# Gate/up bias laid into PSUM by ScalarE, and expert outputs scattered to one DRAM row per (token, choice)

## The chip, the core and the metric

One core of one Trainium2 chip runs the whole program. TensorE (PE), VectorE (DVE), ScalarE (ACT), GpSimd (POOL) and SyncE (SP) each work off an instruction list of their own and wait for each other by semaphores; 16 DMA engines move data between DRAM and SBUF. The metric is the device time of one execution in microseconds (us), smaller is better.

## The reference

Four sequences of 256 tokens, 256 wide. First a causal 16-head attention of the normalised tokens over a context that is keys and values at once, added to `x`. Then a mixture of 16 experts on the normalised result, four experts a token:

```
x = x + attention(layernorm(x), ctx, ctx)
t = layernorm(x)                                   # 1024 tokens
top_val, top_idx = top_k(t @ router_weight.T + router_bias, 4)
score = softmax(top_val)
gate_up = t @ gate_up_proj[e] + gate_up_proj_bias[e]      # 256 -> 512, gate and up interleaved
gate = min(gate, 7); up = clip(up, -7, 7)
out_e = ((up + 1) * gate * sigmoid(1.702 * gate)) @ down_proj[e] + down_proj_bias[e]
x = x + sum over the token's four experts of score_e * out_e
```

## The kernel before

The program has four stages.

**Attention** (to about 108 us). `steps` is one list of units that all engines walk through: `T` transposes, `X` raw scores for the row maxima, `M` the maxima, `S` scores and exponentials, `V` weighing of values, `O` output, `Y` transposes of normalised tokens, `L` router logits, `R` ranks of tokens in their experts. `slot(b)` writes their order for each sequence `b`; the one for the last sequence is changed.

**Routing** (to about 136 us). The 4096 (token, choice) pairs are sorted into at most NB = 47 blocks of 128 slots, each block of one expert. Tables of zeros and single values (`vblk_hot`, `low_hot`) are multiplied on TensorE, and the product gives for every slot the token in it (`slot_tok`); a slot without a token gets a padding row. `down_rows(b)` multiplies scores by the down biases; ACT copies the result into `x_tok`. Normalised tokens with their scores go to `y_rows` in DRAM, and two DRAM tensors, `acc_rows0` and `acc_rows1`, are filled with `x1` (the tokens after attention) and with the bias rows.

**Blocks** (to about 302 us). For each block i POOL gathers 128 rows of `y_rows` by an indirect DMA (ring of 6, `xg`, a part of `ctx_tok`), PE transposes them (`x_turn`), multiplies by the gate/up weights (`gate_up`), DVE and ACT make the activation, PE transposes it (`h_turn`) and multiplies by the down weights (`down`), ACT scales by the score (`weighted`, into `o_sb`, a ring of 3 in `x_tok`), and POOL adds the 128 rows into `acc_rows` of the block's parity by an indirect DMA that adds; it first waits until the add two blocks earlier has landed. On PE the order of iteration i is `gate_up(i)`, `down(i-2)`, `h_turn(i-1)`, `x_turn(i+2)`; on ACT `sigmoid(i)`, `weighted(i-2)`, `h_turned(i-1)`, `x_turned(i+2)`; on POOL add(i), then gather(i+6). The gate/up bias comes from a matmul of its own ahead of the four weight matmuls of a block: a one-hot column picks the expert's row out of `bias_w`, the bias split into three bf16 parts.

**End.** The last LAST = 3 blocks are not scattered: `last_sum` adds them in PSUM by 24 matmuls with one-hot matrices. SP loads both accumulators (8 DMAs of 256 KB), DVE adds them, adds the PSUM sums, and SP writes `out`.

SP issues nearly all plain DMAs in one order. Lines that matter: L1525 bias matmul, L1529 gate/up, L1548 down, L1538 and L1507 transposes, L653 gather, L660 scatter, L1562 `last_sum`, L1482 bias rows, L498 loads of the accumulators, L1235 and L1240 final adds. The lines on which the order rests:

```
for i in range(NB):                       # POOL
    if i < NS: add_rows(i)
    if i + XG < NB: gather(i + XG)
```

## Time and profile before

| | us |
|---|---|
| median of 3 runs | 312.16 |
| lowest, highest | 309.71, 314.52 |
| the profiled execution | 314.45 |
| its span, first to last instruction | 312.70 |

| engine | busy us | share of the span |
|---|---|---|
| PE matmul | 274.2 | 88% |
| POOL | 185.8 | 59% |
| DVE | 179.8 | 57% |
| ACT | 134.4 | 43% |

A busy share is an average over stages; the block stage takes half the span and is the one to read row by row. The profile also has the clock that TensorE was granted (1.0 is 2.4 GHz, 0.5 is 1.2 GHz): it is 1.0 in the block stage and 0.5 over most of 93 to 140 us. Of the chain of work that ended last 61% is PE, 16% DVE, 5% DMA.

### The profile page before, as it was taken

To read this page: it belongs to the slowest core of one execution; us is meant where nothing else is said; L and a number is where in the kernel's file an instruction comes from. 1 tells how busy PE (TensorE), PEld (TensorE's weight loads), DVE (VectorE), ACT (ScalarE), POOL (GpSimd) and SP (SyncE) were. 2 spreads that over 40 slices of the span, in tenths; PEclk is the share of its full clock that TensorE was granted. 3 is DMA by queue.
4 is the path that set the end of the run, shared out by engine and by line. 5 is a ranking of instruction groups with operands and counts; after the bars stand their busy time and mean duration, and the time that the engine had idled before them with its cause. 6 is when DMAs were issued, how large, how long until landed. Compare 5 with 4: busy or idle time off the path is not lost.

```text
span 312.7 us, 5706 instructions
## 1 busy us (share of the span) xinstructions
PE 274.2 (88%) x1548; PEld 184.8 (59%) x1566; DVE 179.8 (57%) x476; ACT 134.4 (43%) x319; POOL 185.8 (59%) x228
## 2 busy tenths in 40 slices
PE   7696897698989868679998998999999999989895
PEld 6665475375576647335565664665666656556584
DVE  3897757966968477305453453544545556656533
ACT  3244564363464368323353443443444434434410
POOL 5873825624436846240876787687787777767300
PEclk9799999999995575559999999999999999999999
DMA  7704230010269395263454445354555545544574
GB/s 238 237 2 129 92 102 2 2 55 0 66 198 332 106 332 190 86 205 123 70 85 90 70 72 89 63 93 75 80 91 72 91 82 75 93 77 70 98 223 134
DMA packets 26877, 34.33 MB, mean 110 GB/s; under 512 B 2800, under 2 KB 21200, under 8 KB 26848
## 3 DMA queue, kind: packets, MB, share of 16 engines
q0 software_dynamic: 8592, 12.32, 24.0%
q1 hardware_dynamic: 17984, 21.39, 20.8%
q8 instruction: 15, 0.25, 0.3%
q10 hardware_dynamic: 272, 0.26, 0.2%
q14 instruction: 14, 0.11, 0.1%
HBM read 23.46 MB, written 10.43 MB: 108 GB/s over the span
## 4 chain that ended last, share of the span: by engine, by line
PE 61%; DVE 16%; issue 8%; DMA 5%; ACT 3%; POOL 3%; SPq 1%; another core or an unknown queue 1%; ACTq 0%; DVEq 0%
PE ps L1529 22%; PE ps L1548 9%; DVE neg_max L909 6%; PE ps L1265 4%; PE ps L1341 4%; PE ps L1562 3%; DMA ctx_tok<-y_rows,slot_tok 3%; PE ps L1507 3%; PE ps L1538 2%; PE ps L1525 2%; PE ps L1284 2%; DMA br_sb<-n_L_ffn_router_bias_dram 2%; PE ps L1343 2%; PE ps L1317 2%; DVE x_tok L941 1%
## 5 line engine op out<-in xcount | busy, mean ns | idle before, releaser
L1529 PE MATMUL ps<-w_all,q_norm 128*128 x188 | 90.3, 603 | 2.9 <-ACT q_norm L823 1.4
L660 POOL DMA_INDIRECT acc_rows<-x_tok,slot_tok x44 | 70.0, 1590 | 34.1 <-ACT x_tok L845 31.6
L1189 DVE TENSOR_SCALAR v_aug<-ps 128x256 f32<-128x256 f32 x47 | 20.0, 425 | 75.7 <-PE ps L1529 48.1
L653 POOL DMA_INDIRECT ctx_tok<-y_rows,slot_tok x47 | 46.6, 992 | 21.8 <-issue 13.7
L829 ACT ACTIVATE v_aug<-v_aug 128x256 f32<-128x256 f32 x47 | 19.6, 418 | 77.5 <-DVE v_aug L1189 77.5
L1548 PEld LDWEIGHTS ps<-w_all,o_t 128*128 128x128 f32 x188 | 35.6, 190 | 25.4 <-issue 22.9
L1529 PEld LDWEIGHTS ps<-w_all,q_norm 128*128 128x128 f32 x188 | 35.6, 194 | 25.0 <-issue 23.2
L1548 PE MATMUL ps<-w_all,o_t 128*128 x188 | 48.3, 380 | 1.1 <-ACT o_t L834 1.1
L564 POOL TENSOR_SCALAR_AFFINE_SELECT w_all<-w_all 128x256 f32<-128x256 f32 (+1 forms) x48 | 23.4, 505 | 37.1 <-ACT w_all L713 36.3
L713 ACT ACTIVATE w_all<-ps 128x512 f32<-128x512 f32 x48 | 25.5, 599 | 23.2 <-PE ps L1317 23.2
L909 DVE TENSOR_REDUCE neg_max<-ps 128x2 f32<-128x512 f32 (+1 forms) x48 | 30.5, 685 | 7.7 <-PE ps L1290 5.0
L845 ACT ACTIVATE x_tok<-ps,ctx_tok 128x256 f32<-128x256 f32 x47 | 22.3, 475 | 19.2 <-PE ps L1548 18.1
L1200 DVE TENSOR_TENSOR v_aug<-v_aug 128x256 f32<-128x256 f32 x47 | 20.0, 426 | 7.2 <-ACT v_aug L829 7.0
L1507 PE MATMUL ps<-ident,ctx_tok 128*128 128x128 f32 x94 | 19.0, 285 | 5.8 <-DMA ctx_tok<-y_rows,slot_tok 5.8
L1207 DVE SCALAR_TENSOR_TENSOR o_t<-v_aug 128x256 f32<-128x256 f32 x47 | 20.0, 426 | 4.3
L823 ACT ACTIVATE q_norm<-ps 128x256 f32<-128x256 f32 x47 | 18.1, 385 | 4.9 <-issue 4.0
L1284 PE MATMUL ps<-k_t,q_t 64*128 64x256 f32 (+1 forms) x128 | 13.4, 303 | 7.1 <-DVE neg_max L909 4.8
L1194 DVE TENSOR_SCALAR v_aug<-ps 128x256 f32<-128x256 f32 x47 | 19.5, 415 | 0.0
L1341 PE MATMUL ps<-w_all,v_aug 128*32 128x256 f32 x128 | 17.9, 450 | 1.5 <-ACT o_t L721 0.8
L1265 PE MATMUL ps<-ident,w_all 128*128 128x128 f32 x128 | 18.6, 295 | 0.0
L1538 PE MATMUL ps<-ident,o_t 128*128 128x128 f32 x94 | 17.9, 273 | 0.0
L834 ACT ACTIVATE o_t<-ps 128x256 f32<-128x256 f32 x47 | 17.7, 376 | 0.0
(160 smaller groups left out, 391.7 us busy)
## 6 DMA issues: line engine op xcount, KB each, us to landing
w_all<-_L_ffn_gate_up_proj_dram SPq DMA_DIRECT2D x16, 512.0 KB, 5.2
w_all<-in_L_ffn_down_proj_dram SPq DMA_DIRECT2D x16, 256.0 KB, 6.1
acc_rows<-x_tok SPq DMA_DIRECT2D x8, 256.0 KB, 8.2
x_tok<-in_x_dram SPq DMA_DIRECT2D x4, 256.0 KB, 4.8
y_ext<-acc_rows SPq DMA_DIRECT2D x4, 256.0 KB, 3.8
vblk_hot<-acc_rows SPq DMA_DIRECT2D x4, 256.0 KB, 3.7
out_dram<-y_ext SPq DMA_DIRECT2D x4, 256.0 KB, 2.2
ctx_tok<-in_ctx_dram SPq DMA_DIRECT2D x3, 256.0 KB, 5.6
```

The lines of the kernel that those rows point to most:

```text
L564: pool.affine_select(out=blk, in_=blk, compare_op=ALU.is_ge, fill=0.0, base=0, pattern=[[0, n], [1, P]], channel_multiplier=-1).then_inc(s ...
L653: pool.indirect_dma_start(out=xg[:, i % XG, :], out_offset=None, in_=y_dram[:, :], in_offset=bass.IndirectOffsetOnAxis(ap=slot_tok[:, i:i ...
L660: pool.indirect_dma_start(out=acc[i % 2][:, :], out_offset=bass.IndirectOffsetOnAxis(ap=slot_tok[:, i:i + 1], axis=0), in_=o_sb[:, i % 3, ...
L713: act.activation(prob[:, u % P_RING, :], ps[:, u % ST_RING, :], ACT.Exp, scale=SC).then_inc(exp_done, 1)
L845: act.activation(o_sb[:, i % 3, :], ps[:, 6 + i % 2, 0:D], ACT.Copy, scale=xg[:, i % XG, bass.ds(e + D, 1)]).then_inc(o_ready, 1)
L909: dve.tensor_reduce(neg_max[:, b % 2, t, p0 // 4, s, p0 % 4:p0 % 4 + np_], ps[:, work_bank(u), :].rearrange("p (a k) -> p a k", k=keys), A ...
L1265: tr = pe.transpose(ps[:, bank, j * P:(j + 1) * P], src[:, b % 2, t, 2 * pair:2 * pair + 2, :].bitcast(F32) .rearrange("p h c -> p (h c)") ...
L1341: pe.matmul(ps[rows, PVB, col:col + S], v_aug[:, b % 2, 0, h, :], p0, start=True, stop=True, skip_group_check=True)
L1507: tr = pe.transpose(ps[:, 2 + i % 2, k * P:(k + 1) * P], xg[:, i % XG, k * P:(k + 1) * P], ident[:, :])
L1529: mm = pe.matmul(o, x_t[:, i % 3, k, :], w_all[:, bass.ds(e, 1), k * 2 * F:(k + 1) * 2 * F].rearrange("p a n -> p (a n)"), start=False, st ...
L1538: tr = pe.transpose(ps[:, 4 + i % 2, f * P:(f + 1) * P], hid[:, i % 2, f * P:(f + 1) * P], ident[:, :])
L1548: mm = pe.matmul(o, hid_t[:, i % 2, f, :], w_all[:, bass.ds(e, 1), at:at + D].rearrange("p a n -> p (a n)"), start=(f == 0), stop=(f == FD ...
```

## The change

**Bias.** `bias_all` holds the bias of all experts in every partition (two DMAs of 2 MB, each with 128 copies of 8 experts' rows). For every block ACT copies the expert's 512 values from SBUF into the PSUM bank, and the weight matmuls add onto it (`start=False`). The bias matmul, its tables, their POOL and DVE work are gone.

```diff
+            def bias_in_bank(i):
+                if i == 0:
+                    act.wait_ge(block_e_ready, 1)
+                    act.wait_ge(bias_in[0], 16)
+                if i == E // 2:
+                    act.wait_ge(bias_in[1], 16)
+                expert.append(act.value_load(block_e[0:1, i:i + 1], min_val=0, max_val=E - 1))
+                fwait(act, u_ready, i - 1)
+                act.activation(ps[:, i % 2, :], bias_all[:, bass.ds(expert[i], 1), :].rearrange("p a n -> p (a n)"),
+                               ACT.Copy).then_inc(bias_put, 1)
...
                 e = pe.value_load(block_e[0:1, i:i + 1], min_val=0, max_val=E - 1)
-                if i < 2:
-                    pe.wait_ge(b_rows_ready, B - 1 + i)
-                fwait(pe, u_ready, i - 1)
                 o = ps[:, i % 2, :]
-                pe.matmul(o, sel_e[:, bass.ds(e, 1)].to_broadcast([P, P]), bias_w[:, :],
-                          start=True, stop=False)
+                pe.wait_ge(bias_put, i + 1)
                 pe.wait_ge(xt_ready, i + 1)
```

**Scatter.** The hot tables now carry the number of the pair and not of the token. From it DVE works out both the token row to gather and the pair's own row in `pair_rows`; empty slots all gather token row 512 and write to rows of their own past the pairs. The indirect DMA copies and does not add, waits for no earlier one, and reads a ring of 4 (`o_sb` moved into `y_ext`). `x_tok` keeps `x1` plus the bias rows, by one identity matmul a tile in `down_rows`.

```diff
-            def add_rows(i):
+            def rows_out(i):
                 pool.wait_ge(o_ready, i + 1)
-                fwait(pool, added[i % 2], 16 * (i // 2))
-                pool.indirect_dma_start(out=acc[i % 2][:, :],
-                                        out_offset=bass.IndirectOffsetOnAxis(ap=slot_tok[:, i:i + 1], axis=0),
-                                        in_=o_sb[:, i % 3, :], in_offset=None, compute_op=ALU.add
-                                        ).then_inc(added[i % 2], 16)
+                pool.indirect_dma_start(out=pair_dram[:, :],
+                                        out_offset=bass.IndirectOffsetOnAxis(ap=slot_row[:, i:i + 1], axis=0),
+                                        in_=o_sb[:, i % O_RING, :], in_offset=None).then_inc(o_out[i % O_RING], 16)
...
                 for t in range(TB):
-                    mm = pe.matmul(ps[:, b % 2, t * D:(t + 1) * D], score_t[0:E, (TB * b + t) % 4, :], b_down[0:E, :],
-                                   start=(t == 0), stop=True, skip_group_check=True)
+                    rows = ps[:, row_bank(b), t * D:(t + 1) * D]
+                    pe.matmul(rows, ident[:, :], x_tok[:, TB * b + t, :], start=(t == 0), stop=False, skip_group_check=True)
+                    mm = pe.matmul(rows, score_t[0:E, (TB * b + t) % 4, :], b_down[0:E, :],
+                                   start=False, stop=True, skip_group_check=True)
```

**End.** SP loads four rows a token, eight DMAs of 512 KB, after the last scatter has landed. POOL adds planes 2 and 3, DVE adds planes 0 and 1 and both halves to `x_tok`.

```diff
-            for s in range(2):
-                sp.wait_ge(added[s], 16 * (NS // 2))
-                for j in range(4):
-                    sp.dma_start(parts[s][:, 2 * j:2 * j + 2, :],
-                                 acc[s][2 * j * P:(2 * j + 2) * P, :].rearrange("(t p) d -> p t d", p=P)
-                                 ).then_inc(back[j], 16)
+            for r in range(O_RING):
+                sp.wait_ge(o_out[r], 16 * len(range(r, NS, O_RING)))
+            for t in range(NT):
+                at = t * TOP_K * P + t // (NT // 2)
+                sp.dma_start(planes[:, t, :, :], pair_dram[at:at + TOP_K * P, :].rearrange("(k p) d -> p k d", p=P)
+                             ).then_inc(back[t // TB], 16)
...
+            def plane_sum(j):
+                rows = slice(2 * j, 2 * j + 2)
+                dve.wait_ge(back[j], 32)
+                step(dve.tensor_tensor(planes[:, rows, 0, :], planes[:, rows, 0, :], planes[:, rows, 1, :], ALU.add))
+                settle()
+                step(dve.tensor_tensor(x_tok[:, rows, :], x_tok[:, rows, :], planes[:, rows, 0, :], ALU.add))
+                dve.wait_ge(halves_ready, j + 1)
+                settle()
+                step(dve.tensor_tensor(x_tok[:, rows, :], x_tok[:, rows, :], planes[:, rows, 2, :], ALU.add))
...
+            for j in range(4):
+                pool.wait_ge(back[j], 32)
+                pool.tensor_tensor(planes[:, 2 * j:2 * j + 2, 2, :], planes[:, 2 * j:2 * j + 2, 2, :],
+                                   planes[:, 2 * j:2 * j + 2, 3, :], ALU.add).then_inc(halves_ready, 1)
```

**Other traffic.** The writes of `x1` and the bias rows (8 DMAs of 256 KB) and of small zero rows are gone. New on SP's queue are four zero fills of `pair_rows` (1 MB each, beside the maxima of sequences 2 and 3) and the two bias loads, one ahead of and one behind the first `y_rows` write. Expert 5's weights load two sequences earlier.

**Order in the last sequence** (K is a part of an L, one tile of router logits):

```diff
                 order = [("S", b, (0,)), ("V", old, (4, 5, 6, 7)), ("Y", 1, (0,)),
-                         ("S", b, (1,)), ("O", old, (0, 1)), ("L", 0, (0,)), ("S", b, (2, 3, 4)),
-                         ("V", b, (0,)), ("Y", 2, (0,)), ("S", b, (5,)), ("R", 0, (0,)),
-                         ("V", b, (1, 2)), ("L", 1, (0,)), ("V", b, (3,)), ("V", b, (4, 5, 6, 7)), ("R", 1, (0,)), ("O", b, (0, 1))]
+                         ("S", b, (1,)), ("O", old, (0, 1)), ("S", b, (2,)), ("K", 0, (0, 1)), ("S", b, (3,)),
+                         ("K", 0, (2,)), ("L", 0, (0,)), ("S", b, (4,)), ("V", b, (0, 1)), ("Y", 2, (0,)),
+                         ("S", b, (5,)), ("V", b, (2, 3)), ("R", 0, (0,)), ("V", b, (4,)), ("K", 1, (4,)),
+                         ("V", b, (5,)), ("L", 1, (0,)), ("V", b, (6, 7)), ("R", 1, (0,)), ("O", b, (0, 1))]
```

How the instructions stand on three engines, before and of the change. PE in the middle of the block stage, from one `gate_up` through the next `down`, before (`sel_e` and `bias_w` are the bias matmul's operands, `q_norm` holds the transposed tokens, `o_t` the activation):

```order
L1525 ISA
L1525 MATMUL ps<-bias_w,sel_e 128x512
L1529 ISA
L1529 MATMUL ps<-w_all,q_norm 128x512
L1529 ISA
L1529 MATMUL ps<-w_all,q_norm 128x512
L1542 TENSOR_LOAD block_e
L1542 ISA x2
L1548 ISA
L1548 MATMUL ps<-w_all,o_t 128x256
```

The same place in the change:

```order
L1555 ISA
L1555 MATMUL ps<-w_all,q_norm 128x512
L1555 ISA
L1555 MATMUL ps<-w_all,q_norm 128x512
L1568 TENSOR_LOAD block_e
L1568 ISA x2
L1574 ISA
L1574 MATMUL ps<-w_all,o_t 128x256
```

The bias matmul and the instruction that gives it its address are gone, the rest stands as before.

ACT, one iteration of the block stage, before (sigmoid, then `weighted`, `h_turned`, `x_turned`):

```order
L829 ACTIVATE v_aug<-v_aug 128x256
L841 TENSOR_LOAD block_e
L841 ISA x2
L845 ISA
L845 ACTIVATE x_tok<-ps,ctx_tok 128x256
L834 ACTIVATE o_t<-ps 128x256
L823 ACTIVATE q_norm<-ps 128x256
```

And in the change:

```order
L836 ACTIVATE v_aug<-v_aug 128x256
L850 ISA
L850 ACTIVATE y_ext<-ps,ctx_tok 128x256
L841 ACTIVATE o_t<-ps 128x256
L830 ACTIVATE q_norm<-ps 128x256
L818 TENSOR_LOAD block_e
L818 ISA x2
L820 ISA
L820 ACTIVATE ps<-bias_all 128x512
```

The load of the expert's number moved behind the four old activations, and a copy of 512 columns into PSUM follows it.

DVE at the end of the program, behind the last block, before:

```order
L1207 SCALAR_TENSOR_TENSOR o_t<-v_aug 128x256
L1235 TENSOR_TENSOR y_ext<-y_ext,vblk_hot 128x512 x4
L1240 TENSOR_TENSOR y_ext<-y_ext,ps 128x512 x4
```

And in the change (the first and the last quarter of the plane sums; `w_all` holds the planes):

```order
L1210 SCALAR_TENSOR_TENSOR o_t<-v_aug 128x256
L1241 TENSOR_TENSOR w_all<-w_all 128x2x256
L1243 TENSOR_TENSOR x_tok<-x_tok,w_all 128x512
L1246 TENSOR_TENSOR x_tok<-x_tok,w_all 128x512
...
L1241 TENSOR_TENSOR w_all<-w_all 128x2x256
L1243 TENSOR_TENSOR x_tok<-x_tok,w_all 128x512
L1246 TENSOR_TENSOR x_tok<-x_tok,w_all 128x512
L1254 TENSOR_TENSOR x_tok<-x_tok,ps 128x512 x4
```

Three adds a quarter stand where one stood, and all four quarters come before the first add from PSUM.

## Rows read from the trace of the kernel before

**Rows 1.** Timeline (start us, us, engine line), PE, one block; rows left out between.
```profile
202.60 0.38 PE L1525 MATMUL ps<-bias_w,sel_e 128*128 128x512 bf16 x1
202.82 1.88 PE L1529 MATMUL ps<-w_all,q_norm 128*128 x4
...
206.05 1.88 PE L1529 MATMUL ps<-w_all,q_norm 128*128 x4
```
**Rows 2.** Timeline, POOL, two scatters and the gather between them.
```profile
182.15 1.59 POOL L660 DMA_INDIRECT acc_rows<-x_tok,slot_tok  x1 [0.30 <-issue]
...
184.05 0.99 POOL L653 DMA_INDIRECT ctx_tok<-y_rows,slot_tok  x1 [0.30 <-issue]
...
185.34 1.59 POOL L660 DMA_INDIRECT acc_rows<-x_tok,slot_tok  x1 [0.30 <-issue]
```
**Rows 3.** Timeline, ACT, the block's last activation and the next sigmoid.
```profile
203.32 0.39 ACT L823 ACTIVATE q_norm<-ps 128x256 f32<-128x256 f32 x1
...
205.19 0.42 ACT L829 ACTIVATE v_aug<-v_aug 128x256 f32<-128x256 f32 x1 [1.49 <-DVE v_aug L1189]
```
**Rows 4.** The page, costliest groups: ACT copies of 128x512 (mean ns, idle before).
```profile
L713 ACT ACTIVATE w_all<-ps 128x512 f32<-128x512 f32 x48 | 25.5, 599 | 23.2 <-PE ps L1317 23.2
```
**Rows 5.** Timeline, PE, the second block's bias matmul at a granted clock of 0.5.
```profile
140.43 0.63 PE L1525 MATMUL ps<-bias_w,sel_e 128*128 128x512 bf16 x1
...
140.86 2.01 PE L1529 MATMUL ps<-w_all,q_norm 128*128 x4
```
**Rows 6.** Timeline, PE, the block with the longest stall.
```profile
187.96 1.88 PE L1529 MATMUL ps<-w_all,q_norm 128*128 x4
...
193.12 1.88 PE L1529 MATMUL ps<-w_all,q_norm 128*128 x4
```
**Rows 7.** Groups of instructions, PE, 145 to 290 us (busy, mean ns | idle before).
```profile
L1507 PE MATMUL ps<-ident,ctx_tok 128*128 128x128 f32 x86 | 16.6, 275 | 2.6 <-DMA ctx_tok<-y_rows,slot_tok 2.6
```
**Rows 8.** The page, DMA queues (packets, MB, share of 16 engines): POOL's and SP's.
```profile
q0 software_dynamic: 8592, 12.32, 24.0%
q1 hardware_dynamic: 17984, 21.39, 20.8%
```
**Rows 9.** Timeline, last sequence: six exponentials, then the first weighing.
```profile
92.81 3.06 ACT L713 ACTIVATE w_all<-ps 128x512 f32<-128x512 f32 x6 [2.45 <-PE ps L1317]
...
95.30 1.07 PE L1341 MATMUL ps<-w_all,v_aug 128*32 128x256 f32 x4 [0.55 <-POOL w_all L564]
```
**Rows 10.** Timeline, routing: bias rows, ranks, slot table, first gather and transpose.
```profile
119.59 2.07 PE L1482 MATMUL ps<-b_down,score_t 16*128 16x256 f32 x4
...
122.34 0.18 PE L1384 MATMUL ps<-mask,before_b 128*128 128x32 bf16 x1 [0.67 <-DVE mask L1030]
...
128.66 0.21 DVE L1111 SCALAR_TENSOR_TENSOR slot_tok<-ps,pad_f 128x48 uint32<-128x48 f32 x1
...
130.39 1.25 POOL L653 DMA_INDIRECT ctx_tok<-y_rows,slot_tok  x1 [7.74 <-DMA y_rows<-y_ext]
...
133.68 0.66 PE L1507 MATMUL ps<-ident,ctx_tok 128*128 128x128 f32 x2 [2.40 <-DMA ctx_tok<-y_rows,slot_tok]
```
**Rows 11.** Windows (PE, PEld, DVE, ACT, POOL busy, granted clock, DMA share, GB/s), late routing.
```profile
116.00:120.00 4.00, 2.92 (x13) 2.35 (x12) 1.75 (x5) 3.51 (x10) 4.00 (x5) 0.50 1.03 364
```
**Rows 12.** Timeline, the end: last scatter, second load issues, last add.
```profile
293.55 1.55 POOL L660 DMA_INDIRECT acc_rows<-x_tok,slot_tok  x1 [1.66 <-ACT x_tok L845]
...
298.30 2.78 SPq L498 DMA_DIRECT2D vblk_hot<-acc_rows  x4
...
309.44 0.69 DVE L1240 TENSOR_TENSOR y_ext<-y_ext,ps 128x512 f32<-128x512 f32 x1 [0.18 <-PE ps L1562]
```
**Rows 13.** Windows, the end: loads of the accumulators (last two numbers: share, GB/s).
```profile
298.00:300.00 2.00, 2.00 (x12) 1.77 (x11) 0.00 (x0) 0.75 (x2) 0.00 (x0) 1.00 0.96 280
```
**Rows 14.** Timeline: adds on POOL and DVE, both from SBUF, at once.
```profile
55.07 1.28 POOL L383 TENSOR_TENSOR w_all<-ctx_tok,w_all 128x512 fp32r<-128x512 f32 x1
55.54 2.51 DVE L941 TENSOR_TENSOR x_tok<-x_tok,attn 128x256 f32<-128x256 f32 x2
```

More of the change, by code:

```diff
@@ L182, in xattn_moe @@
         small_in = sem("small_in")
-        bias_in = sem("bias_in")
+        bias_in = [sem(f"bias_in{j}") for j in range(2)]
+        bias_put = sem("bias_put")
         w_early = sem("w_early")
@@ L475, in y_rows @@
                              y_ext[:, lo:hi, :]).then_inc(y_out, 16)
-            for b in range(B - 1):
-                x1_out(b)
+            biases(0)
             y_rows(0)
+            biases(1)
             sp.wait_ge(pv_done, 2 * B)
@@ L1183, in _ @@
             picks()
+            block_experts()
             slot_tokens()
```

252 lines of the change are left out of this document (126 added, 126 removed).

## Prediction

> **What bounds the kernel now.** I read the windows of 4 to 20 us first, to see the stages, then the timeline of one block engine by engine, then the chain of waits. PE is busy 88% of the span, but what counts is the block stage. There the weight matmuls of successive blocks start 3.23 us apart (202.82 to 206.05) with nothing idle on PE between [rows 1]. So PE sets the pace, and every microsecond taken from PE's work in a block is worth 47. The next engine is close behind: POOL issues a scatter in 1.59 us and a gather in 0.99, with 0.30 idle before each, and two scatters follow each other after 3.19 us when POOL waits for nothing else [rows 2]. ACT has room: its last activation of a block ends at 203.71 and it waits 1.49 us for the next sigmoid's input [rows 3]. At the end, SP issues the second half of its loads only when the last add has landed [rows 12].
>
> **The bias matmul goes.** It starts 0.22 us ahead of the weight matmuls (202.60 to 202.82) [rows 1], and 0.43 us ahead of them at the lower clock (140.43 to 140.86) [rows 5]. I count 45 blocks at 0.22 and two at 0.43: **-10.8 us**. The pace becomes 3.01 us, if nothing else is slower.
>
> On ACT the copy of 128x512 into PSUM is not in this trace; the nearest row is 128x512 out of PSUM, 0.60 us [rows 4]. With 0.3 us for the load of the expert's number ahead of it (the idle time that POOL's dependent instructions show too, [rows 2]) it would run to about 204.6, and the next sigmoid comes at 205.19, or 204.97 at the new pace [rows 3]. Hidden, with 0.4 us to spare; the bank was emptied before, and PE needs the bias one block later. Were the copy dearer by more than that, each excess 0.1 us would cost up to 4.7 us in all. On DVE and POOL the bias tables' work lies in stretches that wait for PE, and I cost their removal at nothing.
>
> **The scatter without an add.** No plain scatter is in the trace. Its cost on POOL lies between a gather of as many rows, 0.99 us, and the adding scatter, 1.59 [rows 2]. I take 0.99: the gather also moves 128 rows between a DRAM row list and 128 partitions, and what sets 1.59 apart is the add, which reads its destination as well. POOL then needs 0.99 + 0.99 + 0.60 = 2.58 us a block, less than 3.01. The point from which POOL decides is a scatter of 3.01 - 1.59 = 1.42 us. The Trainium skill says that one DMA operation of this kind is one pair of descriptors, one to read and one to write (DMA: Bandwidth & Descriptors, section SWDGE vs HWDGE vs iDMA); by that rule a plain scatter is built like a gather, and no row here shows it.
>
> What the quicker POOL brings: some gathers arrive late. The latest of them stretched its block to 5.16 us (187.96 to 193.12), 1.93 over the pace [rows 6]. In 145 to 290 us PE waited 2.6 us for gathers outright [rows 7], and a refill stands behind each wait; with three such stalls I take 4.4 (bounds 2.6, the waits alone, and 5.8, three times 1.93). A scatter 0.6 us shorter starts each gather 0.6 earlier, while the faster pace takes 2 x 0.22 away, since a gather has two blocks of lead. POOL's queue also moved its 12.3 MB at a share of 24.0% where SP's 21.4 MB took 20.8% [rows 8], twice the time a byte, which I put down to the adds; without them the engines are free about 0.5 us earlier. A lead larger by about 0.7 us covers most of these stalls: **-3.7 us**, bounds 0 and -5.8.
>
> **Before the blocks.** In the last sequence the third pair of scores moves ahead of the router logits. The exponentials of that pair gate the first weighing, which starts at 95.30 after waiting for POOL's masks behind a run of ACT that began at 92.81 [rows 9]. With S(2) earlier ACT can begin about 2 us sooner, but PE now has two runs of logits and two more scores ahead of V: **-1.5 us**, bounds 0 and -2.5.
>
> The identity matmuls double the bias rows' work. For sequence 2 that work took 2.07 us from 119.59 for two tiles, and the ranks, on the path to the slot table, start at 122.34 [rows 10]. Doubled it ends at 123.0 to 123.7, later than 122.34 by 0.7 to 1.4: **+0.9 us**. The one for sequence 3 stands where PE waits 2.40 us for the first gather and hides. The longer arithmetic of the slot table (three more dependent DVE instructions, 0.21 us each as the row shows, some 0.6) lies ahead of a gather that waits for the write of `y_rows`, 130.39 against 128.87 [rows 10]: hidden; uncovered, 0.6.
>
> SP's queue carries 4 MB of zeros and 4 MB of biases more and 2.3 MB less. It ran full at 364 GB/s in 116 to 120 us [rows 11], so the extra 5.7 MB are 16 us of full rate. The zeros go out beside sequence 2's and 3's maxima, from 60 us on, and the biases before the first weights of that stretch; the queue should be clear before the last write of `y_rows` at 127. Cost nothing; 2 MB left over at that moment would cost 6 us.
>
> **The end.** The last scatter starts at 293.55, and its add landed 4.75 us later, when SP's loads go out at 298.30 [rows 12]. For the plain one I take 3.5, near the first gather's 3.29 from start to use [rows 10]. A DMA's fixed part I work out from the end: from 310.13, the last add's end, to 312.70 is 2.57 us for 0.26 MB [rows 12], 0.94 of it at 280 GB/s, so 1.6. The planes are 8 x 0.52 = 4.19 MB in rows of 1 KB, as the accumulators were; those ran at 280 GB/s with the engines full [rows 13]: 15.0 us. Landed: 293.55 + 3.5 + 1.6 + 15.0 = 313.65. PE's last sums are done by then (309.44 [rows 12]). Behind the last plane stand three DVE adds of 0.69 us and POOL's one of 1.28; side by side from SBUF these two hold each other up: two DVE adds took 2.51 us beside POOL's [rows 14]. So 3 x 0.69 + 1.28 = 3.35, then four adds from PSUM, 2.76, and the write, 2.57: 322.3 against 312.7, **+9.6 us**. Bounds: planes at 364 GB/s [rows 11] and no contention, +4.8; landing as late as the add did, +10.9.
>
> That figure of the rate has a rule against it: the Trainium skill gives 341 GB/s for a 1 MB load and full rate from 512 bytes on (DMA: Bandwidth & Descriptors, sections Measured and Specifications). By the rule the planes take 12.3 us, an estimate, and the sum would be 2.7 us smaller; by the row it stays.
>
> **Sum.** -10.8 - 3.7 - 1.5 + 0.9 + 9.6 = -5.5 us. The profiled execution took 314.45 (span 312.70), so 308.95; it lay 0.73% over the median of the runs, so against them **306.7**.
>
> **Rivals.** *POOL becomes the bound (chance 0.14).* The plain scatter costs 1.59 all the same, since the row lists are walked in either case. Then the pace is POOL's 3.19: 45 x 0.04 and 0.9 for the first two, -2.7 instead of -10.8; gathers stay late, 0 instead of -3.7; the last scatter lands as late as the add, +1.2. With -1.5 + 0.9 + 9.6 this is +7.5, or **319.6**: slower by 2.4%. For it speaks that POOL is within 0.04 us of PE now [rows 1, 2]; against it that gather and scatter differ at all.
>
> *The clock stays up (0.13).* From 93 to 140 us TensorE was granted 0.50, the 1.2 GHz level, as in [rows 11], after PE had idled ahead of the first weighing [rows 9]. Denser work there could keep 2.4 GHz. The two bias rows would halve and about 3 us of weighing be saved: some -4, **302.7**. Against it: the exponentials still pace that stretch.
>
> *The planes come at the weights' rate (0.10).* 4.19 MB at 364 GB/s [rows 11] is 11.5 us, 3.5 less: **303.2**.
>
> *Gathers come later (0.13).* 47 x 128 - 4096 = 1920 slots are empty and all read one DRAM row. A gather has two blocks of lead, so a microsecond more of landing than the lead covers costs half a microsecond a block. Two microseconds on a dozen half-empty or empty blocks, 0.7 covered, are +8; on the seven that must be quite empty by the reference's inputs, +4: **310.7**.
>
> **How the numbers follow.** The forecast has 0.50 with a range of its own from 302 to 311. Two in ten of everything lie outside 299 to 315: most of POOL's rival and the ends of the others. A measurement of this kernel tells apart about 2%, 6.2 us: faster means below 305.9. The forecast gives 0.20 to that, the clock 0.12, the planes 0.09, late gathers 0.01: 0.42. Slower, above 318.4: POOL's rival 0.09 and 0.01 from the rest. Same: 0.48.
>
> **What would show it.** Weight matmuls 3.01 us apart, no bias matmul; scatter instructions near 0.99 us; ACT's copy near 0.6 us and idle time left before each sigmoid; PE's wait for gathers under 1 us in the stage. At the end, 19 to 21 us from the last scatter's start to the last plane's landing, then 8.7 to the end. Scatters of 1.4 us or more, an ACT without idle time, or planes landing before PE's last sum would make the prediction wrong.

## Result and the profile after

The changed kernel takes **318.47 us** (median of 4 executions, 317.35 to 319.01), the kernel before beside it 311.84 (309.71 to 314.52): ratio **1.0195**, 95% interval 1.0129 to 1.0262. Two repeats gave 1.0301 (1.0237 to 1.0365) and 1.0146 (1.005 to 1.0241). It is slower, by some 2%; 306.7 was predicted, with 302 to 311 as its range. The medians here and below are of all executions of a kernel, while the ratios leave out those that a lower granted clock had slowed. The profiled execution took 317.35 us, its span is 315.6 (before: 314.45 and 312.70).

For all runs I read five moments off the timelines: the start of the transposes of the last attention outputs, the first gather, the first scatter, the last scatter (each by its start), the end of the span. The stretches between them, in us (the second trace of each kernel in brackets):

| stretch | before | after | difference | predicted |
|---|---|---|---|---|
| start to the last output transposes | 108.35 (106.38) | 108.67 (107.08) | +0.3 (+0.7) | -1.5 |
| to the first gather | 22.04 (22.01) | 29.55 (29.53) | **+7.5** | +0.9 |
| to the first scatter | 17.58 (17.62) | 16.66 (16.63) | -1.0 | 0 |
| first to last scatter, 43 intervals | 145.58 (144.58) | 134.64 (133.97) | **-10.9** (-10.6) | -10.8 - 3.7 |
| last scatter to the end | 19.15 (19.11) | 26.08 (26.09) | **+6.9** (+7.0) | +9.6 |
| span | 312.70 (309.7) | 315.6 (313.3) | +2.9 (+3.6) | -5.5 |

The "predicted" column has the whole bias term, -10.8, in the 43 intervals; at 0.21 us each only 9.0 of it can lie there, the rest belongs to the first blocks, in the row above, and the last ones. Measured against predicted, routing is 6.6 us worse, the blocks 3.6 and the last sequence 1.8, while the first blocks are 1.0 better and the end 2.7: together the 8.4 us between -5.5 and +2.9.

The block stage runs at the pace that was forecast, but gains 10.9 us and not 14.5. Timeline of after, one block:

```profile
206.46 1.88 PE L1555 MATMUL ps<-w_all,q_norm 128*128 x4
...
207.08 0.99 POOL L649 DMA_INDIRECT pair_rows<-y_ext,slot_row  x1 [0.74 <-ACT y_ext L850]
...
207.31 0.60 ACT L820 ACTIVATE ps<-bias_all 128x512 f32 x1
...
209.48 1.88 PE L1555 MATMUL ps<-w_all,q_norm 128*128 x4
```

The weight matmuls start 3.02 us apart, where [rows 1] has 3.23 (the mean over the 43 intervals is 3.13, and the block behind the one shown takes 3.96); the plain scatter takes 0.99 on POOL, where [rows 2] has 1.59, and POOL waits; ScalarE's copy takes 0.60 and stands clear of the next sigmoid. POOL's queue, from the page of after:

```profile
q0 software_dynamic: 4368, 12.32, 13.2%
```

Half the packets and about half the share of [rows 8], for the same bytes.

The loss is in routing. Timeline of after:

```profile
112.15 1.22 PE L1511 MATMUL ps<-x_tok,ident 128*128 128x256 f32 x2 [0.68 <-ACT score_t L756]
113.30 1.22 PE L1512 MATMUL ps<-b_down,score_t 16*128 16x256 f32 x2
...
114.48 0.91 DVE L892 TENSOR_SCALAR y_ext<-x_tok,mv,rstd 128x256 f32<-128x256 f32 x2
...
120.20 1.22 PE L1512 MATMUL ps<-b_down,score_t 16*128 16x256 f32 x2
121.35 1.12 PE L1374 MATMUL ps<-ident,y_ext 128*128 128x128 f32 x4
...
130.25 0.21 PE L1407 MATMUL ps<-mask,before_b 128*128 128x32 bf16 x1
...
138.22 1.23 POOL L643 DMA_INDIRECT ctx_tok<-y_rows,slot_tok  x1 [9.72 <-DMA y_rows<-y_ext]
```

The same places of the kernel before:

```profile
111.51 1.99 PE L1482 MATMUL ps<-b_down,score_t 16*128 16x256 f32 x8 [0.68 <-ACT score_t L765]
...
114.16 0.91 DVE L886 TENSOR_SCALAR y_ext<-x_tok,mv,rstd 128x256 f32<-128x256 f32 x2
...
115.22 1.09 PE L1360 MATMUL ps<-ident,y_ext 128*128 128x128 f32 x4 [1.72 <-DVE y_ext L886]
```

The bias rows of sequences 0 and 1 with their identity matmuls (L1511) hold PE from 112.15 to 121.35, 9.2 us for four tiles, where the kernel before needs 2 us and then waits. Two things add up in this: twice the matmuls, and a clock of 0.5 in 112 to 116 us, where the kernel before had 0.95 in 112 to 114. The token transposes of the last sequence (L1374), whose input is ready at 115.4, start 6 us late. Sequence 2's rows, 125.67 to 130.25, put the ranks (L1407) another 1.8 us back: the first gather comes at 138.22 against 130.39 [rows 10].

The end of after, timeline:

```profile
289.52 0.98 POOL L649 DMA_INDIRECT pair_rows<-y_ext,slot_row  x1 [2.59 <-ACT y_ext L850]
...
291.99 6.89 SPq L493 DMA_DIRECT2D w_all<-pair_rows  x8
...
304.02 1.76 DVE L1241 TENSOR_TENSOR w_all<-w_all 128x512 f32<-128x512 f32 x1
305.81 0.69 DVE L1243 TENSOR_TENSOR x_tok<-x_tok,w_all 128x512 f32<-128x512 f32 x1
306.29 1.33 POOL L666 TENSOR_TENSOR w_all<-w_all 128x512 f32<-128x512 f32 x1 [1.06 <-DMA w_all<-pair_rows]
306.61 1.56 DVE L1246 TENSOR_TENSOR x_tok<-x_tok,w_all 128x512 f32<-128x512 f32 x1
...
310.33 2.48 DVE L1254 TENSOR_TENSOR x_tok<-x_tok,ps 128x512 f32<-128x512 f32 x4
```

and the window of after in which only the planes move (the last number is GB/s):

```profile
300.00:302.00 2.00, 2.00 (x12) 1.74 (x11) 1.55 (x3) 0.00 (x0) 1.01 (x1) 1.00 1.09 385
```

The planes came at 385 GB/s, not at the 280 of [rows 13], and landed at 306.3, 16.8 us behind the last scatter's start. DVE had not caught up by then: where one of its adds of 0.69 us starts behind POOL's, it takes 1.56 to 1.79, and 9.3 us are left to the end.

### The profile page after: what moved, and what is told of

Read it like the earlier page. It is cut to its first block, busy times and chain, and to the rows that moved or that the text cites. A ratio compares the mean times of both kernels' runs of the same rounds, so it can differ in the third digit from the quotient of the medians.

```text
span 315.6 us, 5710 instructions
## 1 busy us (share of the span) xinstructions
PE 277.9 (88%) x1529; PEld 179.9 (57%) x1535; DVE 186.2 (59%) x485; ACT 160.8 (51%) x366; POOL 162.8 (52%) x228
## 3 DMA queue, kind: packets, MB, share of 16 engines
q0 software_dynamic: 4368, 12.32, 13.2%
## 4 chain that ended last, share of the span: by engine, by line
PE 67%; DVE 16%; DMA 7%; issue 3%; SPq 2%; ACT 2%; POOL 1%; another core or an unknown queue 1%; DVEq 0%; ACTq 0%; POOLq 0%
PE ps L1555 27%; PE ps L1574 12%; DVE neg_max L915 6%; PE ps L1279 4%; PE ps L1355 4%; PE ps L1538 3%; PE ps L1564 3%; DMA w_all<-pair_rows 2%; PE ps L1512 2%; PE ps L1511 2%; PE ps L1298 2%; DMA br_sb<-n_L_ffn_router_bias_dram 2%; PE ps L1331 2%; PE ps L1357 1%; PE ps L1384 1%
## 5 line engine op out<-in xcount | busy, mean ns | idle before, releaser
L1555 PE MATMUL ps<-w_all,q_norm 128*128 x188 | 91.8, 611 | 2.8 <-issue 1.6
L649 POOL DMA_INDIRECT pair_rows<-y_ext,slot_row x44 | 43.9, 997 | 48.7 <-ACT y_ext L850 48.4
L643 POOL DMA_INDIRECT ctx_tok<-y_rows,slot_tok x47 | 45.8, 974 | 23.7 <-issue 14.0
L1555 PEld LDWEIGHTS ps<-w_all,q_norm 128*128 128x128 f32 x188 | 32.5, 193 | 29.2 <-issue 28.7
L820 ACT ACTIVATE ps<-bias_all 128x512 f32 x47 | 28.3, 601 | 1.5 <-issue 1.3
L850 ACT ACTIVATE y_ext<-ps,ctx_tok 128x256 f32<-128x256 f32 x47 | 22.3, 474 | 9.4 <-PE ps L1574 5.3
L1298 PE MATMUL ps<-qk_t 64*128 64x256 f32 (+1 forms) x128 | 13.3, 303 | 7.2 <-DVE neg_max L915 4.8
```

Of the source, the lines that this page charges most:

```text
L643: pool.indirect_dma_start(out=xg[:, i % XG, :], out_offset=None, in_=y_dram[:, :], in_offset=bass.IndirectOffsetOnAxis(ap=slot_tok[:, i:i ...
L649: pool.indirect_dma_start(out=pair_dram[:, :], out_offset=bass.IndirectOffsetOnAxis(ap=slot_row[:, i:i + 1], axis=0), in_=o_sb[:, i % O_RI ...
L820: act.activation(ps[:, i % 2, :], bias_all[:, bass.ds(expert[i], 1), :].rearrange("p a n -> p (a n)"), ACT.Copy).then_inc(bias_put, 1)
L1555: mm = pe.matmul(o, x_t[:, i % 3, k, :], w_all[:, bass.ds(e, 1), k * 2 * F:(k + 1) * 2 * F].rearrange("p a n -> p (a n)"), start=False, st ...
```

## Experiments

The theory: the identity matmuls hold back routing (A), on a TensorE that is granted 0.5 there. Its rivals: the added traffic on SP's queue (B), the new order of the last sequence (C).

**Without identity matmuls.** DVE adds the bias rows to `x_tok` instead.

```diff
-                    pe.matmul(rows, ident[:, :], x_tok[:, TB * b + t, :], start=(t == 0), stop=False, skip_group_check=True)
...
+                dve.tensor_tensor(rows, rows, ps[:, row_bank(b), :].rearrange("p (t d) -> p t d", t=TB), ALU.add
+                                  ).then_inc(b_rows_ready, 1)
```

> The changed kernel, but the identity matmuls are gone: the down-bias rows are again formed by one matmul a tile, and DVE adds each 128x512 of them to x_tok, late in the routing stage, in place of ScalarE's copies. Theory A (the identity matmuls hold back routing): in the changed kernel the bias rows of sequences 0 and 1 run from 112.15 to 121.35 us on PE, and the transposes of the last sequence's tokens, whose input is ready at 115.4, start behind them at 121.35; the rows of sequence 2 take another 4.58 us ahead of the ranks. Without them the first gather should start near 130.5 instead of 138.22, and the whole take about 7 us less than the changed kernel, 311 us. Rival B (the 8 MB more on SP's queue) and rival C (the new order of the last sequence) both leave the time within 1.5 us of the changed kernel's 318.5.

312.83 us, ratio 1.0108 (1.0046 to 1.0171). Timeline:

```profile
110.92 1.95 PE L1369 MATMUL ps<-ident,o_t 128*128 128x128 f32 x8
...
132.99 1.23 POOL L643 DMA_INDIRECT ctx_tok<-y_rows,slot_tok  x1 [7.63 <-DMA y_rows<-y_ext]
```

The stretch is 22.07 us, that of the kernel before, with the traffic and the new order still in: A is shown, B and C are out. The median fell by 5.6 us, where 7 were expected; the stretch itself fell by 7.5. (The first gather's clock time is 133 and not 130.5 because everything up to 110.92 came later; see the last section.)

**The old order in the last sequence.**

```diff
-                         ("S", b, (1,)), ("O", old, (0, 1)), ("S", b, (2,)), ("K", 0, (0, 1)), ("S", b, (3,)),
+                         ("S", b, (1,)), ("O", old, (0, 1)), ("K", 0, (0, 1, 2)), ("L", 0, (0,)), ("S", b, (2, 3, 4)),
...
```

> The changed kernel with the units of the last sequence in the order of the kernel before. The prediction gave the new order 1.5 us, so going back should cost +1.5. The trace of the changed kernel has the first weighing of the last sequence at 95.29 us, where the kernel before has it at 95.30, which says about 0. If the new order were the cause of the late routing (rival C), going back would save 3 us or more.

318.37 us, ratio 1.0124 (1.0046 to 1.0201). From the first weighing to the last output transposes 13.05 us, as in the kernel before, against 13.38: the new order costs 0.3 us. The total can't be told from that of the changed kernel (1.0124 and 1.0195, the intervals overlap). Routing took 27.28 here, because the clock was 0.67 in 110 to 120 us and not 0.5.

**Masks ahead of rstd.** The timeline of after says why the order brought nothing:

```profile
90.83 1.09 ACT L704 ACTIVATE w_all<-ps 128x512 f32<-128x512 f32 x2 [0.47 <-PE ps L1331]
...
93.32 0.69 POOL L522 TENSOR_TENSOR rstd<-var_eps,small 128x2 f32<-128x2 f32 x1 [2.48 <-DVE var_eps L888]
...
93.96 2.75 POOL L558 TENSOR_SCALAR_AFFINE_SELECT w_all<-w_all 128x512 f32<-128x512 f32 x6
...
95.29 1.20 PE L1355 MATMUL ps<-w_all,v_aug 128*32 128x256 f32 x8 [1.34 <-POOL w_all L558]
```

The third pair's exponentials are ready at 91.9, but their masks stand on POOL behind a small rstd that waits 2.48 us for DVE.

```diff
-                    if n == (1 if b == B - 1 else 4) and b >= 1:
+                    if n == (2 if b == B - 1 else 4) and b >= 1:
                         rsqrt(b - 1, 1)
```

> The changed kernel with one edit: POOL's rstd for sequence 2 stands behind the masks of the third pair of scores, not ahead of them. Theory: the new order of the last sequence brought nothing because POOL's masks stood behind that rstd, whose input comes from DVE at 93.06 us. Then the first weighing of the last sequence starts 1.4 us earlier, 7.4 us behind the second exponentials of that sequence in place of 8.8, and the total falls by about 1.4. Rival: the scores themselves (PE) gate the weighing, and it stays 8.8.

318.89 us; beside it the kernel before had 311.54. From that sequence's second exponentials (90.45) to the first weighing (97.72) 7.27 us in place of 8.77: the step's 1.5 us, shown. The total did not fall, since this trace has the stalls described below. It gave something else: TensorE's clock fell here too (0.50 in 98 to 100 us), but was back at 1.0 from 101 to 116, and the same identity matmuls took little more than half the time. Windows and timeline of this run:

```profile
112.00:116.00 4.00, 4.00 (x15) 2.01 (x16) 3.70 (x13) 1.35 (x3) 2.63 (x3) 1.00 0.94 394
```
```profile
110.67 0.70 PE L1511 MATMUL ps<-x_tok,ident 128*128 128x256 f32 x2 [0.68 <-ACT score_t L756]
...
115.06 0.69 PE L1512 MATMUL ps<-b_down,score_t 16*128 16x256 f32 x2
115.68 0.66 PE L1374 MATMUL ps<-ident,y_ext 128*128 128x128 f32 x4
```

They hold PE for 5.0 us, not 9.2, and the token transposes start 0.7 us behind their input, not 6. The routing stretch is 23.59 us, not 29.55. So the clock decides whether the identity matmuls cost about 1.5 us (against the 22.04 of before) or 7.5.

**What each half of the change brings to the blocks.** One more bf16 matmul of zeros puts back the PE time of the bias matmul:

```diff
+                pe.matmul(o, ones_b[:, :], zeros[:, :].bitcast(BF16), start=False, stop=False, skip_group_check=True)
                 for k in range(KD):
```

> The changed kernel with one more bf16 matmul of 128x512 (of zeros) ahead of each block's gate/up matmuls, as long as the bias matmul that the change removed. If PE sets the pace of the blocks, as predicted, weight matmuls start 3.23 us apart instead of 3.02 and the time rises by 47 x 0.21 = 9.9 us, less what late gathers gain from the slower pace (up to 3): +7 to +10 us. If DVE, ScalarE or POOL sets the pace at 3.02, the rise is under 3 us.

324.36 us, ratio 1.045 (1.0377 to 1.0522): against the changed kernel's 1.0195 +2.5%, 8 us. By the traces only 5.5 of them come from the matmul: first to last scatter takes 140.12 us in place of 134.64. The traced execution had also reached its last output transposes 3.3 us later (112.01 against 108.67), and the added matmuls stand behind that point. 5.5 is less than the 7 expected: at the slower pace 1.2 us of stalls are left (140.12 - 43 x 3.23) where the changed kernel has 4.8. A scatter that adds:

```diff
-                                        in_=o_sb[:, i % O_RING, :], in_offset=None).then_inc(o_out[i % O_RING], 16)
+                                        in_=o_sb[:, i % O_RING, :], in_offset=None, compute_op=ALU.add
+                                        ).then_inc(o_out[i % O_RING], 16)
```

> The changed kernel with an indirect DMA that adds into the zero-filled pair rows in place of the one that copies; nothing waits for an earlier one. If the cheaper scatter is what lets the blocks run at 3.02 us, POOL's 1.59 + 0.99 + 2 x 0.30 = 3.18 us becomes the pace: 43 x 0.16 = 6.9 us, another 1 to 2 for the last add's landing and a few for late gathers: +7 to +12 us. If POOL had room in any case, the rise is that of the landing alone, under 2.5 us.

331.76 us, ratio 1.0741 (1.0664 to 1.0819). The traced execution, 326.94, is the fastest of its four. In it the blocks take 144.71 us, 10.1 more than in the changed kernel, and the end 27.35, 1.3 more. POOL's scatters are 3.19 us apart where POOL waits for nothing else, as foreseen; that is 7 us of the 10, the rest is stalls. And the bias half alone, on the kernel before:

```diff
-                pe.matmul(o, sel_e[:, bass.ds(e, 1)].to_broadcast([P, P]), bias_w[:, :],
-                          start=True, stop=False)
+                pe.wait_ge(bias_put, i + 1)
```

> The kernel before with the bias part of the change alone: ScalarE's copy into PSUM in place of the bias matmul; the scatters still add into the two accumulators, and routing and end are those of the kernel before. Theory A (the two parts need each other): POOL's 1.59 + 0.99 + 2 x 0.30 = 3.18 to 3.19 us becomes the pace, 0.04 less than 3.23, and late gathers stay: first to last scatter takes 143.5 to 145.5 us against 145.58, the total 0 to 2 us less than before. If the bias part paid by itself, the pace would be 3.02 and the total 9 us less.

306.99 us, ratio **0.981** (0.9722 to 0.9897): faster than before by itself, if by little. Its timeline on POOL:

```profile
209.63 1.59 POOL L649 DMA_INDIRECT acc_rows<-x_tok,slot_tok  x1 [0.30 <-issue]
211.52 0.99 POOL L642 DMA_INDIRECT ctx_tok<-y_rows,slot_tok  x1 [0.30 <-issue]
212.82 1.59 POOL L649 DMA_INDIRECT acc_rows<-x_tok,slot_tok  x1 [0.30 <-issue]
```

POOL is the bound at 3.19 us, as foreseen, but the stretch fell by 4.1 us against the first trace of before (3.1 against the second), where I expected at most 2.1: 1.7 for the pace (43 x 0.04), the rest in fewer stalls. From first to last scatter, the run c4_bias_alone_early further down included:

| | adding scatter | plain scatter |
|---|---|---|
| bias matmul, or as much PE work | 145.58, 144.58 (pace 3.23) | 140.12 (3.23) |
| bias copied by ScalarE | 141.51 and 139.83, with a row for every pair 144.71 (3.19) | 134.64, 133.97 (3.02) |

The bias half alone brings 3 to 6 us, the scatter alone 4.5 to 5.5, both about 11. What lengthens the end by 7 us or more is one row for every pair: 26.08 with the plain scatter, 27.35 with the adding one, 18.96 with the bias half alone.

**The end on DVE alone.**

```diff
-                pool.tensor_tensor(planes[:, 2 * j:2 * j + 2, 2, :], planes[:, 2 * j:2 * j + 2, 2, :],
-                                   planes[:, 2 * j:2 * j + 2, 3, :], ALU.add).then_inc(halves_ready, 1)
...
+                step(dve.tensor_tensor(planes[:, rows, 0:2, :], planes[:, rows, 0:2, :], planes[:, rows, 2:4, :], ALU.add))
```

> The changed kernel; DVE alone adds the planes (one add of 128x1024 and two of 128x512 a quarter), POOL none. In the changed kernel DVE's adds of 0.69 us take 1.56 to 1.79 us whenever POOL's add runs beside them, and DVE ends 6.6 us after the last plane has landed (306.2 to 312.8). If the two engines hold each other up, DVE alone is done sooner: from the last scatter's start to the end 24 to 25.3 us in place of 26.1. If they do not, DVE's larger share (2.65 in place of 2.07 us a quarter) makes it 27 to 28.5.

317.83 us, 314.21 for the kernel before beside it; these totals can't tell a difference of 1 us. Last scatter to the end 24.94 us, against 26.08, inside the 24 to 25.3 expected: DVE does 28% more work (2.65 and not 2.07 us a quarter) and is done sooner. The last quarter, timeline of this run:

```profile
309.70 1.23 DVE L1237 TENSOR_TENSOR w_all<-w_all 128x1024 f32<-128x1024 f32 x1
310.96 0.69 DVE L1239 TENSOR_TENSOR w_all<-w_all 128x512 f32<-128x512 f32 x1
311.68 0.69 DVE L1241 TENSOR_TENSOR x_tok<-x_tok,w_all 128x512 f32<-128x512 f32 x1
```

The Trainium skill (GPSIMD Engine Reference, Specifications) says that GpSimd shares its way into SBUF with VectorE and that the two contend where a VectorE instruction has two SBUF inputs. The trace agrees: in the changed kernel the adds with two SBUF inputs take 1.56 to 1.79 us where they start behind POOL's, and 0.69 here, without POOL's.

**A ring of 7 gathers** (`XG = 7`).

> The changed kernel with seven buffers for gathered rows in place of six, so that each gather starts one block, 3.02 us, earlier. First to last scatter takes 134.64 us in the changed kernel, 43 x 3.02 = 129.9 and 4.8 of stalls. If the stalls are gathers that land late, most of the 4.8 goes: 130 to 132 us. If they are something else on PE (instruction or weight delivery), 134 to 135 stays.

324.4 us, ratio 1.0401 (1.0315 to 1.0486); first to last scatter 138.33, worse than with 6. PE waits for no gather any more, yet every third block stalls. From the list of waits of this run, 155 to 290 us (total, times, longest):

```profile
PE ps L1574 <- ACT o_t L841: 4.7, 7, 1.0
...
DVE v_aug L1192 <- remote: 12.0, 4, 3.2
ACT v_aug L836 <- issue: 11.6, 11, 2.2
```

DVE waits up to 3.2 us where 1 is usual, and ScalarE up to 2.2 us for nothing that the profile shows. A later run shows the same pattern with a ring of 6, so this run says nothing about the ring; it says that stalls of this kind are not late gathers.

**Repeats.**

> The kernel before, unchanged, for a second trace of it. Its profiled execution took 314.45 us where the median is 311.8. Theory A (the stages up to the blocks are the same work each time, and what varies between executions is the stretch up to the last sequence's weighing and the stalls in the blocks): from the transposes of the last attention output (108.35 in the first trace) to the first gather 22.0 us, first to last scatter 141 to 146, last scatter to the end 19.1. If routing itself varied by more than 1 us between executions, the comparison of single traces above would be worth little.

312.69 us. 22.01, 144.58 and 19.11 us: the stretches repeat.

> The changed kernel, unchanged, for a second trace. Theory A: the same three stretches as in the first: 29.5 us to the first gather (27.3 where TensorE keeps a higher clock on the way), 134 to 136 from first to last scatter, 26 to the end. Ratio to the kernel before 1.01 to 1.03.

317.72 us, ratio 1.0301: the second trace of the table above.

**A kernel with the faults mended.** The changed kernel with DVE's bias rows, the masks first, DVE's last scores ahead of its last ranks, and at the end PE adding the last quarter of the planes:

```diff
+                if k == LAST - 1:
+                    pe.wait_ge(back[3], 32)
+                    for t in range(NT - TB, NT):
+                        for c in range(TOP_K):
+                            mm = pe.matmul(ps[:, 0, (t % TB) * D:(t % TB + 1) * D], ident[:, :], planes[:, t, c, :],
+                                           start=False, stop=(c == TOP_K - 1), skip_group_check=True)
```

> The changed kernel with four edits: no identity matmuls (DVE adds the bias rows, as in the run e1_dve_rows); at the end DVE alone adds the first three quarters of the planes and PE the last by identity matmuls into the PSUM bank of the last sums; in the last sequence POOL's rstd for sequence 2 stands behind the masks of the third pair of scores and not ahead of them; DVE makes the scores of sequence 3 before its ranks. From stages: -7.5 us in routing, -1.2 to -3.6 at the end, -1 to -1.5 for the first gather no longer waiting for the write of the last scores, 0 to -1 for the masks: 10 to 13 us under the changed kernel, 306 to 308, ratio to the kernel before 0.975 to 0.99. If the two last edits do nothing, ratio 0.985 to 0.995.

303.17 us, ratio **0.9718** (0.9627 to 0.981), a little better than expected. Routing 21.40, blocks 132.92, end 23.83 us.

> The kernel of the run e5_bias_alone with the two edits of order (POOL's masks ahead of its rstd, DVE's last scores ahead of its last ranks). From stages: 1.3 us less ahead of the first gather, which starts at 130.39 where the slot table is ready at 128.87. Ratio to the kernel before 0.972 to 0.985, against 0.981 without them. If it is the slot table's path that these edits lengthen, no gain or a loss of up to 0.8 us.

307.99 us, ratio 0.9896 (0.9842 to 0.995): short of the 0.972 to 0.985 expected and no better than the bias half alone. Routing 21.94 us: 0.1 less than before, not 1.3. First to last scatter 139.83.

> The kernel of the run c3_both_fixed, unchanged, for a second ratio and a second trace. Ratio 0.96 to 0.985. From the exponentials to the first weighing of the last sequence 7.4 us again in place of 8.8; from the first weighing to the last output transposes 10.6 us if the clock is 1.0 there again, 13.4 if it is 0.5.

312.54 us, ratio 1.0035 (0.9976 to 1.0093): the gain of the first run did not repeat. The same kernel on another chip: 7.50 us from exponentials to weighing, 13.31 to the output transposes at a clock of 0.5 (10.59 at 1.0 in the first trace), routing 21.60, end 23.97, all as expected, but 141.92 from first to last scatter. One of its stalls, timeline:

```profile
202.38 1.98 PE L1552 MATMUL ps<-w_all,q_norm 128*128 x4 [0.38 <-issue]
...
205.86 0.42 DVE L1191 TENSOR_SCALAR v_aug<-ps 128x256 f32<-128x256 f32 x1 [3.28 <-PE ps L1552]
```

The weight matmuls end at 204.4 and DVE takes their result at 205.9. From its waits, 150 to 275 us:

```profile
ACT v_aug L823 <- issue: 10.7, 11, 1.6
DVE v_aug L1191 <- remote: 6.3, 2, 3.2
DVE v_aug L1191 <- issue: 5.8, 4, 2.3
```

and from those of the run c3_both_fixed, the one such line:

```profile
DVE v_aug L1191 <- issue: 1.5, 1, 1.5
```

> The kernel of c3_both_fixed and d2_both_fixed_again, unchanged. Its two ratios differ (0.972 and 1.004), and so do its two traces: first to last scatter 132.9 us in one and 141.9 in the other, where every third block stalls by 1.2 to 1.8 us because DVE or ScalarE starts late with its input ready. Theory: the stalls are a state that the block stage falls into at a pace of 3.02 us; then this trace shows either about 133 or 140 to 143, nothing between, and the ratio lies near 0.97 or near 1.0 with it.

304.76 us, ratio **0.9655** (0.9576 to 0.9734), on the chip of the first: 132.77.

> The changed kernel, unchanged, beside the other two on one chip. Its routing stretch (last output transposes to first gather) 29.5 us where TensorE's clock is 0.5 there, 23 to 24 where it is 0.9 or more, as in the run d3_masks_first. First to last scatter 134 or 140 to 143, as the first kernel of this call. Ratio 1.02 to 1.03.

317.44 us, ratio 1.0146, under the 1.02 expected; routing 29.54 at 0.5, blocks 133.81.

> The kernel of c3_both_fixed with one more bf16 matmul of zeros (128x512) ahead of each block's gate/up matmuls, which makes the pace 3.23 us. Theory: at that pace there is room for the late starts and the stalls stay away, as in e2_extra_matmul (140.1 us from first to last scatter, 43 x 3.23 = 138.9): 139 to 141 in any execution. Beside a first kernel in its stalling state (142) the removal of the bias matmul then brings nothing; beside one without stalls (133) it brings 7. Rival: the stalls have nothing to do with the pace and add to it: 147 to 150 beside a stalling first kernel.

308.32 us, ratio 0.9835 (0.9773 to 0.9898), blocks 138.74, which is 43 x 3.23: next to no stalls. Against the 132.77 of the run before, on the same chip, the bias matmul is worth 6.0 us there, 7 were expected. On the chips with late starts the pair e2_extra_matmul (140.12) and d2_both_fixed_again (141.92) says that the removed matmul brings nothing in such an execution; that pair is from two chips, so it is a hint and not shown.

**PE's waits filled.** 32 small matmuls of zeros in PE's waits of routing:

```diff
+            fill(7, 2)
             tokens_t(B - 1)
...
+            pe.wait_ge(block_e_ready, 1)
+            fill(12, 6)
```

> The kernel of the run c3_both_fixed with 32 small bf16 matmuls (128x256, of zeros, into a PSUM bank that nobody reads) in PE's waits of the routing stage: 7 ahead of the last sequence's token transposes (PE waits 2.51 us there), 4 ahead of the last router logits (1.08), 2 ahead of the last ranks (0.52), 7 around the block places (1.21) and 12 ahead of the first gathered rows (1.49). If TensorE's clock is at 0.5 in routing because PE idles there, it rises, and the stretch from the last output transposes to the first gather falls from 21.4 us to 18 to 20. If the clock goes by something else, the clock stays 0.5 and that stretch is 21.4 to 22.5.

312.81 us, ratio 0.9959 (0.9887 to 1.0031), against 1.0035 for the kernel without them beside it: no difference that can be told. The clock rose to 1.0 in 130 to 135 us and 0.92 in 135 to 140 (0.50 and 0.56 without), yet routing took 21.25 us in place of 21.60, where 18 to 20 were expected if the clock rose. So a higher clock that late in routing is worth little.

## Why the prediction was wrong

- **Bias matmul, -10.8: mechanism and pace right, the worth too high.** The pace is 3.02, as said. But the matmul put back costs 5.5 us (e2) and 6.0 (f3 against f1) in the 43 intervals, not 9.0: the rest goes into stalls that the slower pace does not have. Pricing the saved time at every block takes for granted that nothing else shows up at the faster pace.
- **Plain scatter at 0.99: right**, and with it that POOL's rival (0.14) does not come true; e3 and e5 show the 3.19 it would have had. The Trainium skill's rule that one such DMA operation is a pair of descriptors (DMA: Bandwidth & Descriptors, SWDGE vs HWDGE vs iDMA) agrees: scatter 997 ns, gather 974, over the whole trace of after.
- **Late gathers, -3.7: right in kind, and rather too small.** With the bias matmul's work in place the plain scatter takes the stretch from 145.58 and 144.58 to 140.12 (e2), 4.5 to 5.5 us. Of the two terms together, -14.5, came -10.9, because stalls of another kind stand in the changed kernel: 134.64 - 43 x 3.02 = 4.8 us. PE's outright waits for gathers [rows 7] nearly went there, as said. I put down every stall to late gathers, and most of these are not (PE's waits for gathers come to 0.3 us); some 1.5 us of them are fifteen intervals only 0.1 too long, and what causes the rest stays open. The late starts of DVE and ScalarE come on top in other runs (d2), and are not in this trace.
- **Order of the last sequence, -1.5: wrong, +0.3.** The size of the head start was right (d3: 1.5), but I moved the exponentials on PE and ScalarE and did not look at the third engine between them and the weighing. On POOL the masks stood behind an rstd that waits for DVE until 93.3. The queue of that engine had to be followed as well.
- **Identity matmuls, +0.9: the step that failed, and that turned the sign; +7.5.** I costed sequence 2's (0.7 to 1.4; measured 1.8) and sequence 3's (hidden), and left out those of sequences 0 and 1, which stand ahead of the last sequence's token transposes. Their wait in the kernel before, 1.72 us, is all the cover there was, against 7.2 us of added work. No rival had this path either: of the 0.10 given to "slower", 0.09 was POOL's, and that its 319.6 lies near the measured 318.47 is a coincidence. And in the kernel before the old matmuls ran at a high clock (8 records in 1.99 us); where the granted clock is 0.5 a few microseconds on either side, added work has to be costed at 0.5.
- **SP's queue at nothing: right** (e1).
- **The end, +9.6: mechanism right, four terms mis-sized; +7.0.** The planes moved at 385 GB/s, above the 280 of the row and also above the 341 of the page that I weighed against it (the Trainium skill, DMA: Bandwidth & Descriptors, Measured): 4.19 MB in 10.9 us, not 15.0. SP's loads went out 2.5 us after the last scatter's start, not 3.5. Against that, from the first load's issue (291.99) to the last plane's landing (306.29) it took 14.3 us, which leaves 3.4 for the fixed part, not 1.6. And DVE had work left over when the last plane landed, 9.3 us to the end, not 8.7: POOL's help cost more than it gave (e6). That the total is within 3 us is in part luck: the errors have both signs.
- **Rival "the clock stays up", -4: undersized.** It fell in every trace, but came back during the weighing in three (the runs c3_both_fixed, d3_masks_first and f3_fixed_extra_matmul). First weighing to last output transposes takes 10.6 to 10.8 us there and 13.0 to 13.4 at a clock of 0.5, and routing with the identity matmuls 23.6 and 29.5: about 9 us between the two. All three have the masks ahead of the rstd, but so have four others, in which it came back later or not at all; of the twelve traces with the old place of the rstd none shows it. So the order of the masks may have a part in it; that is not shown.
- **Rival "the planes come at the weights' rate", -3.5: true as to the rate**, but the longer fixed part took 1.8 of it back. **"Gathers come later": not seen**, by the same 0.3 us of waits.

The traces sum to +3 us, the medians to +4 to +7. Part of this is which executions were traced: both traces of the changed kernel in the table are the fastest of their four executions, and the first of before is the slowest of its own. The rest I could not place.

## What to carry to other kernels

When work is added to an engine, list every place where it is added and, for each, what stands behind it in that engine's order and how long the engine waits there: 7 us of matmuls "in a stage that waits anyway" were covered by one wait of 1.7. When work is moved ahead, follow each engine between it and its last user, the small helper instructions of GpSimd too. And test the parts of a change apart: here the bias copy alone is 1 to 2% faster than before, while the change as a whole is 2% slower.

## What the runs showed of the hardware

- TensorE's clock falls at different moments in executions of the same program. The first weighing of the last sequence starts at 93.7, 95.3 and 97.7 us in the three traces of the changed kernel, and anywhere from 92.7 to 100.4 over all traces: the clock was 1.0 all the way to 88 us in the second trace of before, but 0.65 in 12 to 16 us in the first, and in the run e2_extra_matmul also 0.79 in 24 to 40 and 0.66 in 64 to 72. In the trace of after it fell to 0.5 between 93 and 94 us, and before that PE had been busy for 5.00 of 5.00 us. Windows:

```profile
88.00:93.00 5.00, 5.00 (x50) 4.21 (x44) 3.48 (x11) 3.99 (x8) 0.89 (x3) 1.00 0.81 264
93.00:94.00 1.00, 0.94 (x6) 0.62 (x6) 0.80 (x6) 0.37 (x2) 0.68 (x2) 0.57 1.06 393
```

PE's wait for the masks begins only at 94, so the wait that my prediction named does not precede the fall. Comparing stretches and not totals takes most of this out: routing repeats within 0.1 us where the clock in it is the same (29.53 to 29.55 in seven traces of kernels with the identity matmuls; 27.28 and 23.59 where it was higher).
- An fp32 matmul of 256 columns shows as two records. The 16 records of bias rows and identity matmuls for four tiles took 5.0 us at a clock of 1.0 and 9.2 at 0.5, 0.31 and 0.58 each; a matmul over 16 partitions costs as much there as one over 128.
- An indirect scatter that adds takes 1.59 us on GpSimd, a plain one 0.99. The queue of the 47 gathers and 44 scatters carried 8592 packets with adding scatters and 4368 with plain ones, both for 12.32 MB. 4368 is 91 x 48; if every gather has 48, an adding scatter has 144, three times a plain one (an estimate from these counts).
- The bias loads, 128 copies of the same rows, ran beside the weights at 422 GB/s over 96 to 108 us of after, where loads of distinct rows reach 364 [rows 11] to 385. (Shorter windows go up to 463, in 100 to 104 us, but show the DMA engines at 1.10 of full, so they are rough.)
- VectorE or ScalarE can start late at an instruction whose input is ready (in d2_both_fixed_again weight matmuls end at 204.4 us and DVE takes their result at 205.9), in about every third block at a pace of 3.02 us. Four traces have it through most of the stage (e7, d1, d2, d3), three in its first part (e1, e4, e6); on the chip of the c and f runs none of four traces at that pace has it. One and the same kernel took 132.9 and 132.8 us there and 141.9 on another chip. What delays them stays open.
